# Rank sums in one PSUM column, edges and score rows requested sooner, eight loads and the exponential table begun ahead in a two-layer graph network kernel

## The chip, the cores and the metric

The kernel runs on one core of one Trainium2 chip. The metric is the device time of one execution in microseconds (us), the median over several runs. Engines are named as in the profile: PE (TensorE), PEld (its weight loads), DVE (VectorE), ACT (ScalarE), POOL (GpSimd) and SP (SyncE, which here only asks for transfers).

## The reference

There are 6250 nodes with 128 channels (x) and 200,000 edges (src, dst), sorted by dst. Two graph layers follow each other, each with a residual and a layer norm:

- Layer 0: the score of an edge is a · leaky_relu([x[src], x[dst]] w); its exponential is divided by the sum over the edges with the same src; the weighted rows x[src] are summed by dst.
- Layer 1: x is projected to 4 heads of 32 channels; the score of an edge is leaky_relu(left[src] + right[dst]) per head; a softmax runs over the edges with the same src; the rows of dst are summed by src; a projected residual is added and elu is applied.

## The kernel before

Nodes form 49 blocks of 128. For each block of dst the edges lie in one window of 128 x 36 entries. The kernel never gathers by index: it makes one-hot matrices and multiplies by them. Its stages come one after the other, each a block of instructions for all engines with a barrier behind it.

1. `load_and_place` (from line 2009) loads the constants and the first two windows of edges (L2032 and `load_windows`, L105), finds where each window starts, and lets ACT's queue ask for all of x (L2046, L2047).
2. `bin_windows` (from L114) sorts the edges of each of the 49 windows by block of src into slots of 128. Per window n, software-pipelined, DVE's order is: `find(n+2)` (block one-hot L202, equal keys L210 and L213), `pick(n+1)` (L223), `place(n)` (lane one-hot L238), once in seven windows `place_keys` (L187 to L194), `fold(n)` (payload, L245, two instructions), `sum_rank(n+1)` (L231). PE's order is: `fill(n-1)` (L317, 36 matmuls of 98 columns), `base(n+2)` (L278, 36 matmuls of 49 columns), `turn_x(n+2)` (L331), `take_off(n)` (L344), `rank(n+1)` (L288 to L306), `turn(n-1)` (L324), `project(n+1)` (L337). ACT's is: `measure_ranks` (L388), `take_raw` (L411, L412), `place_late` (L396), `take_base` (L382), `spread_key` (L372, L376), `take_x` (L425), `take_low` (L433), `spread_rank(n+1)` (L402), `take_bytes` (L418, L419), `take_high` (L429). SP stores the sorted rows of a window to DRAM (L167 to L171) and waits at the end of the stage until all stores have landed.
3. `score_edges` (from L467) computes the exponentials of layer 0 in 25 pairs of windows of 13 steps. SP loads the sorted rows, broadcast to all partitions, in groups (L564); DVE compares them with the partition number (L587).
4. `layer0_sums`, then `norm_and_project` (L1088 on), which norms the nodes, projects them for layer 1 and whose SP asks for the first `LOADS_1` = 3 groups of rows of layer 1 (L1083), then `layer1` (L1214 on): 343 steps; `make(u)` (L1262) turns a loaded group into one-hots, `add_scores` (L1386, L1388) sums scores, `exponent` (L1452) takes the exponential once a block's top is known, `weigh` (L1307) makes the messages.

The rank of an edge in its slot is the sum of two parts: what stands before it in other partitions, picked out of 49 counts, and how many equal keys stand before it in its own row of 36. `rank(n)` adds all of it by identity matmuls into a PSUM tile of 36 x 7 numbers, of which `sum_rank` then adds each seven:

```
for b in range(0, NB, SUB_B):
    w = min(SUB_B, NB - b)
    nc.tensor.matmul(rank_ps[:, :, 0:w], k.ident_b[:], picked[:, :, b:b + w], start=(b == 0), stop=False)
```

`picked` is laid out [128, 36, 49] in bf16, so two neighbours along its 36 are 98 bytes apart. The order of the work is written out by hand with semaphores; no planner is involved.

Of the kernel before, what the change touches and what calls it, by code (L numbers as in the profile page):

```python
# [18 lines left out]
P = 128  # L19
# [73 lines left out]
LOADS_1 = 3  # L93
# [15 lines left out]
def bin_windows(nc, k, PQ, rows, wide_rows, src_rows, X, src, dst):  # L109
    NB, RING, E = NBK, 3, dst.shape[0]  # L110
    LANE_G, BLK_G, SUB_B, SUB_T, SPREADS = 8, 7, 7, 6, 4
# [4 lines left out]
    with Stage(nc) as ctx:  # L116
# [10 lines left out]
        stored = [ctx.semaphore(f"bin_stored{h}") for h in range(2)]  # L127
# [17 lines left out]
        as_bytes, as_rows = sb("bytes", [P, 2, P], mybir.dt.uint8), sb("rows", [P, 2, P], BF16)  # L145
# [12 lines left out]
        with nc.Block() as block:  # L158
            @block.sync
            def _(sp):  # L160
# [3 lines left out]
                for n in range(NB):  # L164
                    sp.wait_ge(s["bytes"], n + 1)
# [6 lines left out]
                    if n % CHUNK == 0 and n // CHUNK + 2 < NB // CHUNK:  # L172
                        c = n // CHUNK + 2
                        sp.wait_ge(s["keyed"], c + 1)
                        load_windows(sp, k, src, dst, edges[:, c % 2], c * CHUNK, slice(0, CHUNK), read[c % 2])
                for h in range(2):
                    sp.wait_ge(stored[h], 80 * ((NB + 1 - h) // 2))

            @block.vector
            def _(dve):  # L180
# [45 lines left out]
                def sum_rank(n):  # L226
                    if n >= 2:
                        dve.wait_ge(s["rank_spread"], n - 1)
                        dve.wait_ge(s["away"], n - 1)
                    dve.wait_ge(s["ranked"], n + 1)  # L230
                    nc.vector.tensor_reduce(rank_sum[:, n % 2, :], rank_ps, AX.X, ALU.add).then_inc(s["rank_summed"], 1)  # L231

# [18 lines left out]
                place_keys(0, slice(0, FIRST), k.first_read, FIRST, k.first_edges)  # L251
                for n in range(-2, NB + 1):
                    if n + 2 < NB:
                        find(n + 2)
                    if 0 <= n + 1 < NB:
                        pick(n + 1)
# [9 lines left out]
                    if 0 <= n + 1 < NB:  # L266
                        sum_rank(n + 1)
# [4 lines left out]
            def _(pe):  # L272
# [8 lines left out]
                def rank(n):  # L281
# [4 lines left out]
                    for b in range(0, NB, SUB_B):  # L286
                        w = min(SUB_B, NB - b)
                        nc.tensor.matmul(rank_ps[:, :, 0:w], k.ident_b[:], picked[:, :, b:b + w], start=(b == 0), stop=False)  # L288
                    eq, counts = same[:, n % 2, :], rank_ps.rearrange("p t j -> p j t")
                    for t in range(0, 18, SUB_T):  # L290
                        nc.tensor.matmul(counts[:, 0:SUB_T, 18:36], k.ident_b[:],
                                         eq[:, t * W_T:(t + SUB_T) * W_T].rearrange("p (i t) -> p i t", t=W_T)[:, :, 18:36],
                                         start=False, stop=False)
                    halves = eq.rearrange("p (h x) -> p h x", h=2)
                    for t in range(0, 9, 3):
                        nc.tensor.matmul(counts[:, 0:3, :].rearrange("p j (h c) -> p h j c", h=2)[:, :, :, 9:18], k.ident_b[:],
                                         halves[:, :, t * W_T:(t + 3) * W_T].rearrange("p h (i t) -> p h i t", t=W_T)[:, :, :, 9:18],
                                         start=False, stop=False)
                    nines = eq.rearrange("p (h x) -> p h x", h=4)
                    for t in range(0, 6, 3):  # L300
                        nc.tensor.matmul(counts[:, 0:3, :].rearrange("p j (h c) -> p h j c", h=4)[:, :, :, t + 3:9], k.ident_b[:],
                                         nines[:, :, t * W_T:(t + 3) * W_T].rearrange("p h (i t) -> p h i t", t=W_T)[:, :, :, t + 3:9],
                                         start=False, stop=False)
                    threes = eq.rearrange("p (h x) -> p h x", h=12)
                    for t in range(2):
                        ins = nc.tensor.matmul(counts[:, 0, :].rearrange("p (h c) -> p h c", h=12)[:, :, t + 1:3], k.ident_b[:],  # L306
                                               threes[:, :, t * W_T + t + 1:t * W_T + 3], start=False, stop=(t == 1))
# [55 lines left out]
            def _(act):  # L363
                def spread_key(n):
                    if n in (0, FIRST, SECOND):
                        act.wait_ge(s["keyed"], 1 + (0, FIRST, SECOND).index(n))
                    elif n % CHUNK == 0:
                        act.wait_ge(s["keyed"], n // CHUNK + 3)
# [23 lines left out]
                def place_late(n):  # L392
# [3 lines left out]
                    nc.scalar.activation(lanes[:, EARLY:W_T], far[:], ACT.Relu, scale=-1.0, bias=k.one_col[:]).then_inc(s["late_lanes"], 1)  # L396

# [36 lines left out]

                spread_key(0)
                spread_key(1)
                for n in range(-2, NB + 1):
# [14 lines left out]
                    if 0 <= n + 1 < NB:  # L452
                        spread_rank(n + 1)
# [6 lines left out]
def score_edges(nc, k, PQ, rows, e0, den_out, flag, edges):  # L460
# [15 lines left out]
    with Stage(nc) as ctx:  # L476
# [9 lines left out]
        loaded = [ctx.semaphore(f"sc_loaded{h}") for h in range(2)]  # L486
        last_loaded = ctx.semaphore("sc_last_loaded")
        last_got = sb("last_rows", [P, R_BYTES], mybir.dt.uint8)
        got = k.spare_bytes[:, 0:2 * 8 * R_BYTES].rearrange("p (g c) -> p g c", g=2)
# [65 lines left out]
        with nc.Block() as block:  # L555
            @block.sync
            def _(sp):
                def load(pair, j, w, to, arrives):
                    of_rows = rows[pair, 16 * j:16 * j + 2 * w]
                    if pair == PAIRS - 1:  # L560
                        to = to.rearrange("p (a n l) -> p a n l", n=2, l=P)[:, :, 0, :]
                        sp.dma_start(to, of_rows[:, 0, :].partition_broadcast(P)).then_inc(arrives, 16)
                    else:
                        sp.dma_start(to, of_rows.rearrange("a n l -> (a n l)").partition_broadcast(P)).then_inc(arrives, 16)  # L564

                for pair in range(PAIRS):
                    for j in range(6):
# [4 lines left out]
                        load(pair, j, 8, got[:, j % 2], loaded[j % 2])  # L572
                    if pair >= 1:
                        sp.wait_ge(s["hot"], last_group_step(pair - 1, 6) + 1)
                    load(pair, 6, 1, last_got[:], last_loaded)
# [505 lines left out]
def load_rows(sp, k, got, wide_rows, u):  # L1081
    b, g = divmod(u, NBK // GX)
    sp.dma_start(got[:, u % LOADS_1].rearrange("p a x -> p (a x)"),  # L1083
                 wide_rows[g, 2 * b:2 * b + 2].rearrange("a i l -> (a i l)").partition_broadcast(P)
                 ).then_inc(k.rows_loaded[u % LOADS_1], 16)


def norm_and_project(nc, k, X, mean_var, hp, R, got, wide_rows):  # L1088
# [3 lines left out]
    with Stage(nc) as ctx:  # L1092
# [121 lines left out]
def layer1(nc, k, hp, got, wide_rows, spare, X, S, den4):  # L1214
    NB, PER, AHEAD = NBK, NBK // GX, 9
    R = NB * PER
    RING, LOADS = AHEAD + 2, LOADS_1
    CW, HP, FIRST = C + HEADS, 3 * HEADS, 28
    SPLIT, F32R = 3, mybir.dt.float32r
    with Stage(nc) as ctx:  # L1220
# [9 lines left out]
        loaded = k.rows_loaded  # L1230
# [3 lines left out]
        absent, never = sb("absent", [P, 2, NB], BF16), sb("never", [P, P], BF16)  # L1234
# [9 lines left out]
        with nc.Block() as block:  # L1244
            @block.sync
            def _(sp):
                for u in range(LOADS, R):
                    sp.wait_ge(s["hot"], u - LOADS + 1)
                    load_rows(sp, k, got, wide_rows, u)

            @block.vector
            def _(dve):
                ch = Chain(dve, s["chain"])

                def make(u):
                    dve.wait_ge(loaded[u % LOADS], 16 * (u // LOADS + 1))
# [1232 lines left out]
```

## Time and profile before

| | us |
|---|---|
| median of 3 runs | 3279.44 |
| lowest and highest | 3279.33, 3297.03 |
| the profiled execution | 3298.39 |
| its span | 3296.6 |

The page divides the span into 40 slices of 82.4 us. Sorting the windows fills the first five slices, the scores of layer 0 run up to the sixteenth, the sums of layer 0 to the twenty-seventh, layer 1 follows.

```profile
## 2 busy tenths in 40 slices
PE   5777699999999999699999999988999999999995
DVE  8999889999999997799999999988999999999996
ACT  6988788888888885799999999976888888888886
PEclk9988899999999997799999999998999999999998
```

Each digit is the busy share of a slice in tenths (9 is 90% or more); PEclk is the TensorE clock that was granted, in tenths of full speed.

### The profile page before, as it was taken

What the parts mean: (1) busy time and instruction counts of PE and PEld (TensorE: products, weight loads), DVE (VectorE), ACT (ScalarE), POOL (GpSimd) and SP (SyncE); (2) the same over time, 40 slices, a digit from 0 to 9 for tenths busy, and PEclk for the clock granted to TensorE, in tenths of its full rate; (3) what the DMA queues carried; (4) which work ended last, traced back from release to release, by engine and by line L of the source; (5) the groups of instructions that cost most, each with busy time, mean ns of one, the idle gap of its engine ahead of it and who ended that gap; (6) DMA issues with size and microseconds to landing.
All of it is one profiled execution on the core that took longest, in us unless ns stands there. A gap on an engine that the chain in (4) does not pass through costs nothing. (4 is left out here: it accounts for less than half of the span.)

```text
span 3296.6 us, 101505 instructions
## 1 busy us (share of the span) xinstructions
PE 3064.1 (93%) x40072; PEld 2795.8 (85%) x40072; DVE 3045.2 (92%) x4914; ACT 2749.8 (83%) x6951; POOL 155.1 (5%) x251
## 2 busy tenths in 40 slices
PE   5777699999999999699999999988999999999995
PEld 4666577777778777699999999988999999999993
DVE  8999889999999997799999999988999999999996
ACT  6988788888888885799999999976888888888886
POOL 0000000000000000000000000000111111111110
PEclk9988899999999997799999999998999999999998
DMA  2000022222222222233333333325554555555541
GB/s 66 13 13 12 10 103 93 92 86 92 93 91 93 92 87 47 65 97 97 97 97 97 96 97 96 97 58 162 161 163 160 163 163 161 162 164 163 160 141 41
DMA packets 173135, 333.06 MB, mean 101 GB/s; under 512 B 54860, under 2 KB 108704, under 8 KB 172576
## 3 DMA queue, kind: packets, MB, share of 16 engines
q1 hardware_dynamic: 170996, 323.30, 32.2%
q8 instruction: 322, 5.28, 0.6%
q10 hardware_dynamic: 1660, 3.20, 0.4%
q14 instruction: 157, 1.29, 0.1%
HBM read 320.77 MB, written 5.66 MB: 99 GB/s over the span
## 5 line engine op out<-in xcount | busy, mean ns | idle before, releaser
L987 PE MATMUL l_gathered<-xp,l_src_onehot 128*128 128x128 bf16 x7203 | 467.0, 221 | 11.2 <-DVE l_src_onehot L900 11.2
L1398 PE MATMUL l_gathered<-hp,l_onehot 128*128 128x128 bf16 x7203 | 458.9, 219 | 0.0
L682 PE MATMUL sc_z<-sc_onehot,pq 128*128 128x256 f32 (+1 forms) x2450 | 429.4, 298 | 27.6 <-DVE sc_leaky L595 18.3
L987 PEld LDWEIGHTS l_gathered<-xp,l_src_onehot 128*128 128x128 bf16 x7203 | 407.9, 99 | 26.4 <-DVE l_src_onehot L900 11.7
L766 ACT ACTIVATE sc_leaky<-sc_z 128x1024 f32<-128x1024 f32 (+3 forms) x325 | 309.4, 952 | 142.4 <-PE sc_z L686 139.5
L595 DVE SCALAR_TENSOR_TENSOR sc_leaky<-sc_z,sc_leaky 128x1024 f32<-128x1024 f32 (+3 forms) x325 | 370.1, 1139 | 59.9 <-ACT sc_leaky L766 52.3
L825 DVE TENSOR_TENSOR l_lane<-iota_b,l_lane_pairs 128x896 bf16<-128x896 bf16 x686 | 420.7, 613 | 0.0
L1398 PEld LDWEIGHTS l_gathered<-hp,l_onehot 128*128 128x128 bf16 x7203 | 406.6, 98 | 0.4
L686 PE MATMUL sc_z<-sc_onehot,pq 128*128 128x256 f32 (+1 forms) x2450 | 401.0, 286 | 0.0
L1412 PE MATMUL l_acc<-e,l_lane_wide 128*128 128x132 f32 x2744 | 385.3, 283 | 0.7 <-ACT e L1476 0.6
L682 PEld LDWEIGHTS sc_z<-sc_onehot,pq 128*128 128x128 f32 x2450 | 344.6, 196 | 40.2 <-issue 38.8
L686 PEld LDWEIGHTS sc_z<-sc_onehot,pq 128*128 128x128 f32 x2450 | 344.1, 195 | 0.0
L1307 DVE TENSOR_TENSOR e<-l_gathered,l_weight 128x768 f32<-128x768 f32 x343 | 325.5, 949 | 12.7 <-issue 9.0
L1412 PEld LDWEIGHTS l_acc<-e,l_lane_wide 128*128 128x128 f32 x2744 | 335.7, 190 | 1.6 <-ACT e L1476 1.0
L1465 ACT CAST l_lane_wide<-l_lane 128x896 fp32r<-128x896 bf16 x343 | 328.9, 959 | 0.0
L1033 ACT CAST l_lane_wide<-l_lane 128x896 fp32r<-128x896 bf16 x343 | 322.3, 940 | 4.0 <-DVE l_lane L825 4.0
L1470 ACT CAST l_message_halves<-e 128x396 fp32r<-128x396 f32 x343 | 179.1, 522 | 159.8 <-DVE e L1307 157.5
L998 PE MATMUL l_acc<-l_messages,l_lane_wide 128*128 128x128 f32 x2058 | 305.9, 285 | 5.7 <-ACT l_messages L1042 5.7
L587 DVE TENSOR_SCALAR sc_onehot<-placed,part 128x1536 fp32r<-128x1536 uint8 (+1 forms) x300 | 298.8, 997 | 3.4 <-DMA placed<-edge_rows 3.3
L1042 ACT ACTIVATE l_messages<-l_gathered,e 128x128 f32<-128x128 f32 x1029 | 300.5, 362 | 0.0
L914 DVE TENSOR_TENSOR l_message_halves<-l_messages,l_message_halves 128x512 fp32r<-128x512 f32 x343 | 237.3, 692 | 53.1 <-ACT l_message_halves L1048 48.0
L1476 ACT ACTIVATE e<-l_gathered,l_weight 128x32 f32<-128x32 f32 x1372 | 279.4, 285 | 0.0
(242 smaller groups left out, 6114.5 us busy)
## 6 DMA issues: line engine op xcount, KB each, us to landing
rows_got<-edge_rows_wide SPq DMA_DIRECT2D x343, 448.0 KB, 3.7
l_got<-edge_rows_src SPq DMA_DIRECT2D x343, 224.0 KB, 3.2
placed<-edge_rows SPq DMA_DIRECT2D x144, 512.0 KB, 3.7
out_dram<-X SPq DMA_DIRECT2D x12, 256.0 KB
edge_rows<-bin_bytes SPq DMA_DIRECT2D x98, 6.1 KB
edge_rows_wide<-bin_rows SPq DMA_DIRECT2D x98, 12.2 KB
sc_last_rows<-edge_rows SPq DMA_DIRECT2D x24, 64.0 KB, 3.5
placed<-edge_rows SPq DMA_DIRECT2D x6, 256.0 KB, 4.0
```

Source lines behind the costliest of these rows:

```text
L595: nc.vector.scalar_tensor_tensor(out=y, in0=z, scalar=ALPHA, in1=y, op0=ALU.mult, op1=ALU.add).then_inc(s["leaky"], 1)
L682: nc.tensor.matmul(z[:, b, 0:nw, :], PQ[:, b0 + b, q, 0:C], hot[:, r % HOTS, b, 0, 0:nw, :], start=(b == u and q == 0), stop=False)
L686: ins = nc.tensor.matmul(z[:, u:u + v, n, :], PQ[:, 2 * pair + n, q, C:2 * C], hot[:, r % HOTS, u:u + v, 1, n, :], start=False, stop=(n == ...
L766: nc.scalar.activation(y, z, ACT.Relu, scale=1.0 - ALPHA).then_inc(s["positive"], 1)
L825: return nc.vector.tensor_tensor(out.rearrange("p i (u v) -> p i u v", v=2), k.iota_b[:].rearrange("p (u v) -> p u v", v=2).unsqueeze(1).t ...
L987: ins = nc.tensor.matmul(gps[:, t % 2, i * P:(i + 1) * P], hot[:, t % RING, i, :], parts[:, g * GX + i, q, :], start=(q == 0), stop=(q == 2))
L998: nc.tensor.matmul(acc[:, n % 2, 0:C], lane_wide[:, t % 2, i, :].bitcast(F32), msg[:, t % 2, i, :], start=(g == 0 and i == SPLIT), stop=Fa ...
L1033: nc.scalar.copy(lane_wide[:, t % 2], lane[:, t % 2]).then_inc(s["lane_wide"], 1)
L1307: nc.vector.tensor_tensor(msg[:, t % 2, 0:w, 0:C].rearrange("p i (e d) -> p i e d", e=HEADS), gps[:, t % 2, 0:w * P].rearrange("p (i e d) ...
L1398: ins = nc.tensor.matmul(gps[:, t % 2, i * P:(i + 1) * P], dst_hot[:, t % RING, i, :], hp[:, g * GX + i, q, 0:C], start=(q == 0), stop=(q ...
L1412: nc.tensor.matmul(acc[:, b % 2, 0:CW], lane_wide[:, t % 2, i, :].bitcast(F32), msg[:, t % 2, i, :], start=(g == 0 and i == SPLIT), stop=F ...
L1465: nc.scalar.copy(lane_wide[:, t % 2], lane[:, t % 2]).then_inc(s["lane_wide"], 1)
```

## The change

In `bin_windows` the rank sums go into one number per edge: 49 + 18 + 9 + 6 + 2 = 84 matmuls of 12 to 36 columns in place of 17 of 12 to 252; `sum_rank` on DVE goes, and ACT copies the 36 sums out of PSUM (`take_rank`) ahead of `spread_rank`. The first window's keys are placed as soon as that window is there; x is asked for in two parts, the first seven blocks in the first stage and the rest by ACT's queue at the start of `bin_windows`. SP asks for the first two groups of score rows ahead of the last window's stores, and the wait for those stores moves into the scoring stage, ahead of pair 22. `norm_and_project` asks for eight groups of layer 1, five of them into a part of S that is written only later; `layer1` opens with one exponential of a constant column on ACT.

```diff
-        rank_ps = ps("rank_ps", [P, 512])[:, 0:SUB_B * W_T].rearrange("p (t j) -> p t j", j=SUB_B)
+        rank_ps = ps("rank_ps", [P, 512])[:, 0:W_T]
...
                 for n in range(NB):
+                    if n == NB - 1:
+                        sp.wait_ge(s["key_spread"], NB)
+                        sp.wait_ge(s["spread"], NB)
+                        sp.wait_ge(s["same"], NB)
+                        for h in range(2):
+                            sp.wait_ge(stored[h], 80 * (NB // 2))
+                        for j in range(2):
+                            load_score_rows(sp, k, rows, 0, j, 8, score_rows(k)[:, j], k.score_rows[j])
                     sp.wait_ge(s["bytes"], n + 1)
...
-                for h in range(2):
-                    sp.wait_ge(stored[h], 80 * ((NB + 1 - h) // 2))
...
-                def sum_rank(n):
...
-                    nc.vector.tensor_reduce(rank_sum[:, n % 2, :], rank_ps, AX.X, ALU.add).then_inc(s["rank_summed"], 1)
...
-                place_keys(0, slice(0, FIRST), k.first_read, FIRST, k.first_edges)
+                place_keys(0, slice(0, 1), k.zero_read, 1, k.first_edges)
                 for n in range(-2, NB + 1):
                     if n + 2 < NB:
                         find(n + 2)
+                    if n == -2:
+                        place_keys(0, slice(1, FIRST), k.first_read, FIRST - 1, k.first_edges)
...
-                    for b in range(0, NB, SUB_B):
-                        w = min(SUB_B, NB - b)
-                        nc.tensor.matmul(rank_ps[:, :, 0:w], k.ident_b[:], picked[:, :, b:b + w], start=(b == 0), stop=False)
-                    eq, counts = same[:, n % 2, :], rank_ps.rearrange("p t j -> p j t")
-                    for t in range(0, 18, SUB_T):
...
+                    for b in range(NB):
+                        nc.tensor.matmul(rank_ps, k.ident_b[:], picked[:, :, b], start=(b == 0), stop=False)
+                    eq = same[:, n % 2, :]
+                    for t in range(18):
+                        nc.tensor.matmul(rank_ps[:, 18:36], k.ident_b[:], eq[:, t * W_T + 18:t * W_T + 36], start=False, stop=False)
...
                 def turn_x(n):
                     if n == 0:
+                        pe.wait_ge(k.x_first, 16)
+                    if n == CHUNK:
                         pe.wait_ge(k.x_loaded, 32)
...
+                def take_rank(n):
+                    if n >= 2:
+                        act.wait_ge(s["rank_spread"], n - 1)
+                        act.wait_ge(s["away"], n - 1)
+                    act.wait_ge(s["ranked"], n + 1)
+                    nc.scalar.copy(rank_sum[:, n % 2, :], rank_ps).then_inc(s["rank_summed"], 1)
...
+                full = x.shape[0] // P
+                act.dma_start(X[:, CHUNK:full, :], x[CHUNK * P:full * P].rearrange("(b p) c -> p b c", p=P)).then_inc(k.x_loaded, 16)
                 spread_key(0)
...
                     if 0 <= n + 1 < NB:
+                        take_rank(n + 1)
                         spread_rank(n + 1)
...
+def rows_ahead(S):
+    return S[:, 10:45, :].rearrange("p b c -> p (b c)").bitcast(BF16).rearrange("p (u a x) -> p u a x", u=AHEAD_1, a=2)
...
-                for u in range(LOADS_1):
-                    load_rows(sp, k, got, wide_rows, u)
+                for u in range(LOADS_1 + AHEAD_1):
+                    load_rows(sp, k, got, S, wide_rows, u)
...
-                for u in range(LOADS, R):
-                    sp.wait_ge(s["hot"], u - LOADS + 1)
-                    load_rows(sp, k, got, wide_rows, u)
+                for u in range(LOADS_1 + AHEAD_1, R):
+                    turn = (u - LOADS_1 - AHEAD_1) // LOADS_1
+                    sp.wait_ge(s["hot"], u - LOADS_1 + 1 if turn else u - LOADS_1 - AHEAD_1 + 1)
+                    load_rows(sp, k, got, S, wide_rows, u)
...
+                nc.scalar.activation(exp_ready[:], k.one_col[:], ACT.Exp)
                 find_absent(0)
...
-                act.dma_start(X[:, 0:NFULL, :], x[0:NFULL * P].rearrange("(b p) c -> p b c", p=P)).then_inc(k.x_loaded, 16)
+                act.dma_start(X[:, 0:CHUNK, :], x[0:CHUNK * P].rearrange("(b p) c -> p b c", p=P)).then_inc(k.x_first, 16)
```

## Rows read from the trace of the kernel before

**Rows 1.** The page: busy time over the span, share of it, instructions.

```profile
PE 3064.1 (93%) x40072; PEld 2795.8 (85%) x40072; DVE 3045.2 (92%) x4914; ACT 2749.8 (83%) x6951; POOL 155.1 (5%) x251
```

**Rows 2.** Windows: stretch, its length, busy (instructions) per engine, PEclk, DMA share, GB/s.

```profile
165.00:247.00 82.00, 60.95 (x991) 52.93 (x991) 81.25 (x102) 71.80 (x236) 0.00 (x0) 0.90 0.08 13
```

**Rows 3.** Timeline of DVE, one window sorted: start, length, engine, line, operation.

```profile
152.72 0.41 DVE L231 TENSOR_REDUCE bin_rank_sum<-bin_rank_ps 128x36 f32<-128x252 f32 x1
153.05 1.19 DVE L202 TENSOR_TENSOR bin_onehot<-iota_b,e 128x1764 bf16<-128x1764 bf16 x1
...
155.82 2.01 DVE L238 TENSOR_TENSOR bin_lanes<-iota_b,bin_rank 128x3584 bf16<-128x3584 bf16 x1
...
159.99 0.41 DVE L231 TENSOR_REDUCE bin_rank_sum<-bin_rank_ps 128x36 f32<-128x252 f32 x1
```

**Rows 4.** Timeline of DVE: the first and the last of the 49 L202.

```profile
22.72 1.21 DVE L202 TENSOR_TENSOR bin_onehot<-iota_b,e 128x1764 bf16<-128x1764 bf16 x1 [1.07 <-ACT e L372]
...
381.16 1.20 DVE L202 TENSOR_TENSOR bin_onehot<-iota_b,e 128x1764 bf16<-128x1764 bf16 x1
```

**Rows 5.** Timeline of PE, the same window; in brackets the idle time before.

```profile
153.05 1.78 PE L317 MATMUL bin_slots<-bin_payload,bin_lanes 128*128 128x98 bf16 x36 [2.07 <-DVE bin_payload L245]
154.68 1.10 PE L278 MATMUL bin_base<-bin_onehot,above_b 128*128 128x49 bf16 x36
155.61 0.30 PE L331 MATMUL bin_x_turned_ps<-ident,X 128*128 128x128 f32 x1
...
156.00 1.13 PE L288 MATMUL bin_rank_ps<-bin_picked,ident_b 128*128 128x252 bf16 x7
156.96 0.44 PE L291 MATMUL bin_rank_ps<-bin_same,ident_b 128*128 128x108 bf16 x3
...
157.53 0.24 PE L324 MATMUL bin_turned<-ident_b,bin_raw 128*98 128x128 bf16 x1
157.60 0.65 PE L337 MATMUL bin_product<-w_ext,bin_x_turned 128*128 128x256 f32 x2
```

**Rows 6.** Timeline of ACT, the same window.

```profile
153.22 0.38 ACT L402 CAST bin_rank<-bin_rank_sum 128x224 bf16<-128x224 f32 x1 [0.49 <-DVE bin_rank_sum L231]
...
157.82 0.21 ACT L382 CAST bin_base_sum<-bin_base 128x49 bf16<-128x49 f32 x1
```

**Rows 7.** Timelines of PE and of DVE at the lower clock.

```profile
169.63 3.10 PE L317 MATMUL bin_slots<-bin_payload,bin_lanes 128*128 128x98 bf16 x36 [4.11 <-DVE bin_payload L245]
...
172.77 2.03 DVE L238 TENSOR_TENSOR bin_lanes<-iota_b,bin_rank 128x3584 bf16<-128x3584 bf16 x1 [0.30 <-PE bin_slots L317]
```

**Rows 8.** Timelines of ACT and DVE, and windows, at the start of the sorting.

```profile
14.42 1.28 ACT L372 ACT_TABLE_LOAD   x1 [6.72 <-PEq L60]
...
20.37 0.20 DVE L187 TENSOR_SCALAR bin_block_of<-e 128x72 int32<-128x72 int32 x1 [5.65 <-DMA e<-in_dst_dram]
...
33.18 2.02 DVE L238 TENSOR_TENSOR bin_lanes<-iota_b,bin_rank 128x3584 bf16<-128x3584 bf16 x1
...
16.00:18.00 2.00, 0.00 (x0) 0.00 (x0) 0.00 (x0) 0.00 (x0) 0.00 (x0) 1.00 1.06 285
```

**Rows 9.** From sorting to scoring: timeline of DVE; SP's waits (total, times, longest).

```profile
414.68 1.95 DVE L587 TENSOR_SCALAR sc_onehot<-placed,part 128x1536 fp32r<-128x1536 uint8 x2 [3.32 <-DMA placed<-edge_rows]
...
SPq L158 <- DMA edge_rows_src<-bin_rows: 0.9, 1, 0.9
```

**Rows 10.** Start of layer 1: DVE's waits for its loads; timelines of ACT and DVE.

```profile
DVE l_onehot L1262 <- DMA rows_got<-edge_rows_wide: 7.3, 7, 2.3
...
2252.53 1.28 ACT L1452 ACT_TABLE_LOAD   x1
...
2254.39 0.96 DVE L1307 TENSOR_TENSOR e<-l_gathered,l_weight 128x768 f32<-128x768 f32 x1 [0.47 <-ACT l_weight L1452]
```

**Rows 11.** Windows: the end of the scoring.

```profile
1290.00:1300.00 10.00, 10.00 (x65) 8.74 (x67) 4.46 (x10) 5.14 (x18) 0.00 (x0) 0.50 0.22 34
```

More of the change, by code:

```diff
@@ L92 @@
 GX = 7
-LOADS_1 = 3
+LOADS_1, AHEAD_1 = 3, 5
 R_BYTES = 4 * P
@@ L144, in bin_windows @@
         raw = sb("raw", [P, 2, 2 * NB], BF16)
-        as_bytes, as_rows = sb("bytes", [P, 2, P], mybir.dt.uint8), sb("rows", [P, 2, P], BF16)
+        late = e0[:].rearrange("p a b -> p (a b)")[:, 2304:2496]
+        as_bytes = late[:, 0:64].bitcast(mybir.dt.uint8).rearrange("p (h l) -> p h l", h=2)
+        as_rows = late[:, 64:192].bitcast(BF16).rearrange("p (h l) -> p h l", h=2)
         xt = sb("x_turned", [P, 2, C])
         base_ps = ps("base", [P, 512])[:, 0:NB]
-        rank_ps = ps("rank_ps", [P, 512])[:, 0:SUB_B * W_T].rearrange("p (t j) -> p t j", j=SUB_B)
+        rank_ps = ps("rank_ps", [P, 512])[:, 0:W_T]
         slots_ps = ps("slots", [P, 512])[:, 0:2 * NB]
@@ L294, in rank @@
+                    eq = same[:, n % 2, :]
+                    for t in range(18):
+                        nc.tensor.matmul(rank_ps[:, 18:36], k.ident_b[:], eq[:, t * W_T + 18:t * W_T + 36], start=False, stop=False)
                     halves = eq.rearrange("p (h x) -> p h x", h=2)
[L295 to L298, printed above, removed]
+                    for t in range(9):
+                        nc.tensor.matmul(rank_ps.rearrange("p (h c) -> p h c", h=2)[:, :, 9:18], k.ident_b[:],
+                                         halves[:, :, t * W_T + 9:t * W_T + 18], start=False, stop=False)
@@ L299, in rank @@
                     nines = eq.rearrange("p (h x) -> p h x", h=4)
[L300 to L303, printed above, removed]
+                    for t in range(6):
+                        c = t // 3 * 3 + 3
+                        nc.tensor.matmul(rank_ps.rearrange("p (h c) -> p h c", h=4)[:, :, c:9], k.ident_b[:],
+                                         nines[:, :, t * W_T + c:t * W_T + 9], start=False, stop=False)
@@ L557, in _ @@
             def _(sp):
[L558 to L564, printed above, removed]
                 for pair in range(PAIRS):
-                    for j in range(6):
+                    if pair == PAIRS - 3:
+                        for h in range(2):
+                            sp.wait_ge(k.stored[h], 80 * ((NB + 1 - h) // 2))
+                    for j in range(2 if pair == 0 else 0, 6):
                         if pair >= 1 or j >= 2:
@@ L571, in _ @@
                             sp.wait_ge(s["away"], late_steps(used + 1))
-                        load(pair, j, 8, got[:, j % 2], loaded[j % 2])
+                        load_score_rows(sp, k, rows, pair, j, 8, got[:, j % 2], loaded[j % 2])
                     if pair >= 1:
                         sp.wait_ge(s["hot"], last_group_step(pair - 1, 6) + 1)
-                    load(pair, 6, 1, last_got[:], last_loaded)
+                    load_score_rows(sp, k, rows, pair, 6, 1, last_got[:], last_loaded)
             @block.vector
@@ L1255, in make @@
                 def make(u):
-                    dve.wait_ge(loaded[u % LOADS], 16 * (u // LOADS + 1))
+                    rows, arrived, count = place_of_rows(k, got, S, u)
+                    dve.wait_ge(arrived, count)
                     if u >= RING:
```

76 lines of the change are left out of this document (43 added, 33 removed).

## Prediction

> **What bounds the kernel now.** The page first: PE and DVE are each busy for over nine tenths of the span [rows 1], so no one engine is the answer and each stage must be read by itself. The change touches one long stage, the sorting of the 49 windows, and three seams: the start, the step from sorting to scoring, the start of layer 1. The sums of layer 0 and the body of layer 1 are left as they are. In the sorting stage DVE is busy for 81.25 of 82 us, PE for 61 and ACT for 72 [rows 2]: DVE bounds it. The timeline of one window shows how. DVE comes round in 159.99 - 152.72 = 7.27 us with no gap [rows 3]; PE is idle for 2.07 us of that, waiting for the payload [rows 5], and ACT for 0.49 us, waiting for the rank sum [rows 6]. Over the stage, with the keys of a new chunk in every seventh window, the mean is (381.16 - 22.72) / 48 = 7.47 us [rows 4].
>
> **The rank sum leaves DVE.** L231 runs 0.41 us but the next instruction starts 0.33 us behind it [rows 3], so 0.33 us is what it costs. It goes 49 times. Twice at the end and once at the start DVE waits for another engine just behind it, so I count 46: 46 x 0.33 = **15.2 us**, if neither PE nor ACT takes over at 7.27 - 0.33 = 6.94 us.
>
> ACT gets a copy out of PSUM much like L382, 0.21 us [rows 6], and `spread_rank` must wait for its result, so I charge 0.25 us. ACT's round is 7.27 - 0.49 + 0.25 = 7.03 us. That is over 6.94 in a plain window and under the mean of 7.47 - 0.33 = 7.14. It may slip by 0.09 us in each of six windows and catches up when DVE places keys. `place` reads the spread rank about 2.2 us after it is made now (155.82 against 153.22 + 0.38) [rows 3, 6], so the slip is covered: nothing. The copy stands where the wait stood, and PE has the sum ready long before (157.53 against ACT's arrival near 160).
>
> PE is the open question. The rank matmuls take 157.53 - 156.00 = 1.53 us now; seven wide ones take 0.96 of it, 137 ns each for 252 columns [rows 5]. Afterwards 49 matmuls read 36 columns each, every column 98 bytes from the last, and 35 more read short contiguous stretches. For the 35 I take 26 ns each, the spacing of L278 ((155.61 - 154.68) / 36) [rows 5]: 0.91 us. The 49 are not in the trace. Their lower bound is the same 26 ns. Their upper bound is 137 ns: L288 too makes 36 jumps of 98 bytes, and picks up seven columns after each. Between them I reason from what L288 pays for its jumps. L317 streams 98 columns in (154.68 - 153.05) / 36 = 45 ns, 0.46 ns a column, so 252 columns should take 116 ns, or 105 at 2.4 GHz; the excess is 21 to 32 ns for 36 jumps. Add 36 columns (17 or 15 ns) and a narrow one costs 38 to 47 ns; I take 45, near the upper of the two. The rank part is then 49 x 0.045 + 0.91 = 3.1 us, up 1.6.
>
> Does PE still fit? From L317's start to the end of L337 it now spends 5.2 us [rows 5], of which 0.3 is a wait for `pick` that DVE's earlier arrival removes. The rest without rank is 5.2 - 0.3 - 1.53 = 3.35 us, so the round is 4.26 + 49c, with c the price of a narrow matmul in us. At c = 0.045 it is 6.46, under 6.94 by 0.48; PE takes over at c = 55 ns. The 67 extra weight loads run beside the matmuls, as in L278's spacing.
>
> The slack is thin where the clock is low. The granted clock is 0.90 on average in this stage [rows 2], so the lower of the two levels (1.2 of 2.4 GHz) holds for a fifth of it. There L317 takes 3.10 us instead of 1.78, and DVE already waits 0.30 us for it [rows 7]. A fifth of 350 us at half speed is up to 35 us of PE work that comes late. PE's idle 2.07 us a window swallows that today; afterwards 49 x 0.48 = 23 us of slack are left, so at most 12 us come through. With PE idle for less of each window the clock may also fall less often, which would make it nothing. I take off **5 us**, a little under the middle.
>
> The Trainium skill speaks against this part. Its page "SBUF — State Buffer", section "Door 1: The DMA port swizzle", says that reads run at full rate only while they stay in a 16-byte line, at least two to a line, and that each step to a new line pays. Each column here is in a line of its own. The 137 ns of L288 agree that jumps cost; the page has no size for it. Its page "TensorE: Matmul & The Clock Gate", section "Wait — 56ns, not 53.3ns?", gives a floor of about 25 ns however narrow; by that alone all 84 would take an estimated 2.1 us and the 5 us above would mostly stay.
>
> **The start.** DVE sits idle for 5.65 us until the second window of edges lands at 20.37 [rows 8]. The new code places the first window at 14.5, but ACT first issues a transfer and loads its table (1.28 us, from 14.42) [rows 8], so it can spread keys only near 16.6, and `find(0)` starts near 17.7 in place of 22.7. Placing keys in two parts and waiting for ACT between them gives back 2.5 us. The later windows, asked for from 15.3 on, now queue with the 2.7 MB of x that were issued beside them; at 285 GB/s [rows 8] that is 9.5 us, so windows 2 and 3 land near 25.5 when DVE wants them at 24.5. I find the first `place` near 31.0 against 33.18 [rows 8]: **2.2 us**, between 1 and 3.3 (queue hides nothing or costs nothing).
>
> **From sorting to scoring.** DVE waits 3.32 us for the first rows, and SP had waited 0.9 us for the last stores to land before anyone could leave the stage [rows 9]. Both go: **4.2 us**. The two loads (512 KB each) are asked for near 404 and land near 408, before DVE is ready. SP's new waits stand ahead of the last window's stores, but all they wait for is over before those rows exist near 407, so nothing queued behind is late. The moved wait for the stores is met hundreds of us earlier: nothing. Late next is the start of the constants and barriers, which stays.
>
> **Start of layer 1.** DVE waits 7.3 us in all for its first loads, 6.7 of it ahead of the first block's top [rows 10]. With eight there these waits go. But ACT now loads the table before it finds the absent slots, which PE's first scores wait for: 0.7 us late. The table load of 1.28 us stands on the path to the first weights at 2254.39 [rows 10] and leaves it; the gather that ends near 2253.1 allows 1.2 of it. Together 6.7 - 0.7 + 1.2 = 7.2; I take **7.0 us**, between 6 and 8. Five more issues on SP and 2.2 MB more lie in the projection stage, where the core moves almost nothing. Later loads are asked for by the same rule as before.
>
> **Sum.** 15.2 - 5 + 2.2 + 4.2 + 7.0 = 23.6 us. The profiled execution took 3298.4 (span 3296.6), so it would take 3274.8. It stood 19 us above the median of the runs; from that median, 3279.4 - 23.6 = **3255.8 us**. A measurement of this kernel can tell about 1% (33 us) from no change, so this is "within 1%".
>
> **Rivals.**
> - *PE takes over and the kernel gets slower.* Place: the 49 narrow matmuls. The seams give 13.4 us, 0.27 a window, so the loss begins where 4.26 + 49c passes 7.47 + 0.27, at c = 71 ns. Halfway between my 45 and the bound of 137, at c = 90 ns, the round is 8.67 us: 49 x 1.20 = 59 us lost, less 13.4, gives 3279.4 + 45.4 = 3325. For it: the jumps and L288's price. Against it: 36 columns are a seventh of L288's. Chance 0.12. By the SBUF page's rule this is the direction. Between 55 and 71 ns the time lies from 3262 to 3279: 0.16.
> - *The clock decides the rest.* PE is full for 10 us of 10 at half clock at the end of the scoring [rows 11]. The runs differ by 17.7 us (3297.03 against 3279.33). If the moved seams put most runs in the longer case, the median is 3255.8 + 18 = 3274: 0.12.
> - *Everything goes well.* PE's slack holds and each seam gives its upper value: 15.2 + 3.3 + 4.2 + 8 = 30.7, so 3249, and a little less if low-clock waits of today go too: 0.12.
> - Forecast, 3250 to 3262: 0.48.
>
> **Range and chances.** 3247 to 3286 takes in the forecast, the good case, the clock case and the balanced PE; it leaves out the dear narrow matmul. Faster by over 1% (under 3246.6) needs more than all upper values: 0.10. Slower by over 1% (over 3312) needs c above 85 ns: 0.10. Within 1%: 0.80.
>
> **What would show it.** Right: L231 gone, DVE's round 6.9 to 7.0 us in plain windows; the spacing of the 36-column matmuls near 45 ns; PE's wait for the payload down to about 0.5 us; DVE's gap ahead of L187 under 1 us; no wait of DVE for the first score rows; the first weights of layer 1 in ACT without a table load. Wrong: a spacing above 55 ns, with DVE waiting for `bin_slots` in most windows; a long wait for windows 2 and 3 behind x; table loads that come back between the first exponential and the weights.

## The result, and the profile after

The kernel became slower: 3388.0 us (median of 5 runs, 3384.1 to 3391.0) against 3279.4 (5 runs), a ratio of 1.032 with a 95% interval of 1.030 to 1.035. The profiled execution took 3387.84, its span 3386.0; the one of before took 3298.39, 19 us above its median, and this execution holds those 19 us in one place, the scoring (last section).

First the page of after: busy time over the span, and the slices, to be read against [rows 1] and the slices of before.

```profile
PE 3263.5 (96%) x43355; PEld 3018.4 (89%) x43355; DVE 3041.4 (90%) x4872; ACT 2771.9 (82%) x7001; POOL 154.2 (5%) x251
...
PE   7999998999999999889999999998999999999995
...
DVE  7777777999999999889999999997999999999997
...
PEclk8666668999999999889999999998999999999998
```

PE has 199 us more to do and DVE 4 us less. Sorting now fills over six slices in place of nearly five; in them DVE is at 0.7 and PE full, and the granted clock, 0.9 and 0.8 before, is 0.6. The windows of after over the stretch of [rows 2] say the same (stretch, length, busy and instructions of PE, PEld, DVE, ACT, POOL, PEclk, DMA share, GB/s). The second row lies on the 36 matmuls of one `fill`:

```profile
165.00:247.00 82.00, 82.00 (x1292) 78.78 (x1290) 59.65 (x64) 57.67 (x186) 0.00 (x0) 0.67 0.06 11
...
159.30:162.30 3.00, 3.00 (x38) 3.00 (x37) 0.85 (x1) 2.89 (x11) 0.00 (x0) 0.50 0.09 17
```

PE is busy for 82.00 of 82 us where it was for 60.95. One window in the timeline of DVE (start, length, engine, line, operation; in brackets the idle time before and what ended it):

```profile
152.24 2.03 DVE L252 TENSOR_TENSOR bin_lanes<-iota_b,bin_rank 128x3584 bf16<-128x3584 bf16 x1 [2.33 <-PE bin_slots L327]
...
158.41 0.33 DVE L231 TENSOR_TENSOR bin_same<-e,placed 128x324 bf16<-128x324 bf16 x1 [0.61 <-PE bin_rank_ps L316]
...
159.06 1.09 DVE L244 TENSOR_TENSOR bin_picked<-bin_onehot,bin_base_sum 128x1764 bf16<-128x1764 bf16 x1
162.49 2.02 DVE L252 TENSOR_TENSOR bin_lanes<-iota_b,bin_rank 128x3584 bf16<-128x3584 bf16 x1 [2.33 <-PE bin_slots L327]
```

DVE comes round in 162.49 - 152.24 = 10.25 us, where it took 7.27 without a gap [rows 3]. The reduction is gone, and two waits for PE stand in the round: 2.33 us for `fill`, 0.61 us for `rank`. The timeline of PE shows what they wait for, to be held against [rows 5]:

```profile
153.35 4.09 PE L301 MATMUL bin_rank_ps<-bin_picked,ident_b 128*128 128x36 bf16 x49
157.26 0.65 PE L304 MATMUL bin_rank_ps<-bin_same,ident_b 128*128 128x18 bf16 x18
...
158.34 1.17 PE L349 MATMUL bin_product<-w_ext,bin_x_turned 128*128 128x256 f32 x2
159.30 3.15 PE L327 MATMUL bin_slots<-bin_payload,bin_lanes 128*128 128x98 bf16 x36
162.25 1.24 PE L292 MATMUL bin_base<-bin_onehot,above_b 128*128 128x49 bf16 x36
```

No bracket is left: PE never waits. The 49 narrow matmuls stand (157.26 - 153.35) / 49 = 80 ns apart. The 36 of `fill` take 3.15 us in each of the windows between 67 and 380 us, at a granted clock of 0.50, where most took 1.78 before [rows 5]. In steps of 1 us the clock is 1.00 over the first of the narrow matmuls (163.20 to 165.20), 0.50 from 166.20 on, through the last third of them, `project` and `fill`, and on the way up again (0.79 from 162.20 to 163.20) while `base` runs. The waits of `place` between 40 and 380 us, in total, times and longest, say how general this is:

```profile
DVE bin_lanes L252 <- PE bin_slots L327: 70.7, 34, 2.3
```

From the first `place` to the end of the last payload it is 524.16 - 30.95 = 493.2 us, against 402.17 - 33.18 = 369.0: **124.2 us lost**, 2.53 in each of 49 windows. The seams, of DVE's and ACT's timelines after, to be held against [rows 8 to 10]:

```profile
25.06 0.20 DVE L208 TENSOR_SCALAR bin_block_of<-bin_edges 128x72 int32<-128x72 int32 x1 [1.00 <-DMA bin_edges<-in_dst_dram]
...
30.95 2.02 DVE L252 TENSOR_TENSOR bin_lanes<-iota_b,bin_rank 128x3584 bf16<-128x3584 bf16 x1
...
532.28 1.02 DVE L604 TENSOR_SCALAR sc_onehot<-placed,part 128x1536 fp32r<-128x1536 uint8 x1
...
2345.85 0.46 ACT L1483 ACTIVATE l_weight<-l_score,l_negated 128x196 f32<-128x196 f32 x1
...
2346.57 0.96 DVE L1338 TENSOR_TENSOR e<-l_gathered,l_weight 128x768 f32<-128x768 f32 x1
```

The first `place` stands at 30.95 and stood at 33.18: 2.2 us. From the last payload to the first make of the scores it is 532.28 - 524.16 = 8.1 us in place of 414.68 - 402.17 = 12.5: 4.4. From the start of the norm (2293.74, before 2194.10) to the first messages it is 52.8 us in place of 60.3: 7.5, and the exponential at 2345.85 has no table load ahead of it. Against the median of before, 124.2 - 2.2 - 4.4 - 7.5 = 110 us; measured were 108.6.

### The profile page after: what moved, and what is told of

It is laid out like the page before. It is cut to its first block and busy times, and to the rows that moved or that the text cites. A ratio compares the mean times of both kernels' runs of the same rounds, so it can differ in the third digit from the quotient of the medians.

```text
span 3386.0 us, 108082 instructions
## 1 busy us (share of the span) xinstructions
PE 3263.5 (96%) x43355; PEld 3018.4 (89%) x43355; DVE 3041.4 (90%) x4872; ACT 2771.9 (82%) x7001; POOL 154.2 (5%) x251
## 5 line engine op out<-in xcount | busy, mean ns | idle before, releaser
L699 PE MATMUL sc_z<-sc_onehot,pq 128*128 128x256 f32 (+1 forms) x2450 | 419.7, 293 | 23.2 <-DVE sc_leaky L612 18.0
L1004 PEld LDWEIGHTS l_gathered<-xp,l_src_onehot 128*128 128x128 bf16 x7203 | 407.9, 99 | 26.3 <-DVE l_src_onehot L917 11.7
L703 PE MATMUL sc_z<-sc_onehot,pq 128*128 128x256 f32 (+1 forms) x2450 | 393.9, 282 | 0.0
L699 PEld LDWEIGHTS sc_z<-sc_onehot,pq 128*128 128x128 f32 x2450 | 334.5, 191 | 35.4 <-issue 34.1
L703 PEld LDWEIGHTS sc_z<-sc_onehot,pq 128*128 128x128 f32 x2450 | 338.1, 192 | 0.0
L1338 DVE TENSOR_TENSOR e<-l_gathered,l_weight 128x768 f32<-128x768 f32 x343 | 326.0, 950 | 12.5 <-issue 9.0
```

What stands on the lines that cost most here:

```text
L699: nc.tensor.matmul(z[:, b, 0:nw, :], PQ[:, b0 + b, q, 0:C], hot[:, r % HOTS, b, 0, 0:nw, :], start=(b == u and q == 0), stop=False)
L703: ins = nc.tensor.matmul(z[:, u:u + v, n, :], PQ[:, 2 * pair + n, q, C:2 * C], hot[:, r % HOTS, u:u + v, 1, n, :], start=False, stop=(n == ...
L1004: ins = nc.tensor.matmul(gps[:, t % 2, i * P:(i + 1) * P], hot[:, t % RING, i, :], parts[:, g * GX + i, q, :], start=(q == 0), stop=(q == 2))
L1338: nc.vector.tensor_tensor(msg[:, t % 2, 0:w, 0:C].rearrange("p i (e d) -> p i e d", e=HEADS), gps[:, t % 2, 0:w * P].rearrange("p (i e d) ...
```

## The experiments

Theory A: a narrow matmul is dear because each of its columns lies in another small piece of SBUF (the chip's on-chip memory, from which PE reads); PE becomes the bound, and its clock, which falls in this stage, makes it worse. Rivals: the number of matmuls or their weight loads is what costs (B); a seam hurts something later (C).

**Each half by itself.** `seams_only` keeps the sums and `sum_rank` of before; `rank_only` is before with the new sums alone.

```diff
 # seams_only: after, but (shortened)
-        rank_ps = ps("rank_ps", [P, 512])[:, 0:W_T]
+        rank_ps = ps("rank_ps", [P, 512])[:, 0:SUB_B * W_T].rearrange("p (t j) -> p t j", j=SUB_B)
...
-                        take_rank(n + 1)
+                        sum_rank(n + 1)
```

> The changed kernel with the rank sums as they were (17 wide matmuls and the sum on DVE); all of the seams stay changed. If the loss is all in the rank sums, the seams give what their rows show after the change (2.2 us at the start, 4.4 from sorting to scoring, 7.5 at the start of layer 1): 3279.4 - 14 = 3265, and the sorting goes back to 7.27 us a plain window. If the seams carry part of the loss (x asked for in two parts, loads ahead of the last stores), the time is above 3279.

> The kernel before with the rank sums of the changed one alone. If the rank sums carry all of the loss and the seams are apart from it: 3388 + 14 = 3402, windows of 10.25 us as in the changed kernel. If the two work on each other (the earlier start shifting the clock, say), it differs from that by more than 5 us.

Measured: seams only 3265.4 us (10 runs, 3264.4 to 3267.1) against 3279.1, ratio 0.9945 (0.9926 to 0.9965); rank only 3403.8, ratio 1.036 (1.032 to 1.040). So the seams give 13.7 and the sums cost 124.7; together 111, near the 108.6 of the whole. That speaks against C: nothing later is hurt. In seams only the stretch of [rows 2] reads as before:

```profile
165.00:247.00 82.00, 62.69 (x1033) 54.52 (x1034) 81.58 (x95) 72.35 (x235) 0.00 (x0) 0.90 0.08 14
```

Seams only is also the fastest version here, half a per cent under before, with an interval that leaves out 1.

**The price of a jump, by itself.** `step_probe` adds rows of 48 equal matmuls on a zeroed tile to the first stage of the kernel before, one row for each step between columns. (One execution, 3308.4 us, of which only these rows are read.) In short form, not the code itself, with columns, step of reading and step of writing:

```diff
+ for cols, step, out in [(128,1,1),(36,1,1),(36,2,1),(36,4,1),(36,8,1),(36,16,1),(36,49,1),(18,49,1),(72,8,1),(36,1,7),(72,1,7),(128,1,1)]:
+     for _ in range(48):
+         nc.tensor.matmul(tried[cols, out elements apart], k.ident_b[:], zero[cols, step elements apart], start=True, stop=True)
```

> The kernel before with series of 48 extra matmuls at the end of the first stage, each of a row of zeros, with one price to read from each: the spacing. Theory A (each new 16-byte piece of SBUF that the moving operand touches costs a fixed 2.2 ns): 36 columns that lie 2, 4, 8, 16, 32, 98 bytes apart take 26, 26, 40, 80, 80, 80 ns, 18 columns 98 bytes apart take 40, 72 columns 16 bytes apart 160. Theory B (any step over one element costs the same): 80 ns from 4 bytes on. Theory C (a matmul in a long row of narrow ones pays a fixed sum): 18 columns cost as much as 36. PSUM columns written 28 bytes apart: 30 ns for 36 and 60 for 72, if 0.84 ns a column from the rank sums of before holds. The whole time only shows the series' own length, some 30 to 40 us more.

Measured, in the timeline of PE (two bytes an element; the order is that of the list):

```profile
16.61 1.36 PE L2122 MATMUL tried_psum<-tried_zero,ident_b 128*128 128x36 bf16 x48
17.81 1.35 PE L2124 MATMUL tried_psum<-tried_zero,ident_b 128*128 128x36 bf16 x48
19.01 1.85 PE L2126 MATMUL tried_psum<-tried_zero,ident_b 128*128 128x36 bf16 x48
20.69 1.77 PE L2128 MATMUL tried_psum<-tried_zero,ident_b 128*128 128x36 bf16 x24
23.06 1.76 PE L2128 MATMUL tried_psum<-tried_zero,ident_b 128*128 128x36 bf16 x24 [0.60 <-issue]
24.65 3.44 PE L2130 MATMUL tried_psum<-tried_zero,ident_b 128*128 128x36 bf16 x48
27.91 4.02 PE L2132 MATMUL tried_psum<-tried_zero,ident_b 128*128 128x36 bf16 x48
31.75 2.42 PE L2134 MATMUL tried_psum<-tried_zero,ident_b 128*128 128x18 bf16 x48
33.99 6.42 PE L2136 MATMUL tried_psum<-tried_zero,ident_b 128*128 128x72 bf16 x48
...
42.90 3.17 PE L2140 MATMUL tried_psum<-tried_zero,ident_b 128*128 128x72 bf16 x48
45.87 2.88 PE L2142 MATMUL tried_psum<-tried_zero,ident_b 128*128 128x128 bf16 x48
```

From one row's start to the next, divided by 48 (for 16 bytes by 24, from 23.06 to 24.65), 36 columns cost 25 ns when 2 or 4 bytes apart, 35 at 8 bytes, 66 at 16, 68 at 32 and 80 at 98. At 16 and 32 bytes that is about 1.9 ns a column, at 98 bytes 2.2; 18 columns at 98 bytes cost 47 ns and 72 columns at 16 bytes 130. The unit that fits is a piece of 16 bytes: with 8 bytes between columns there are half as many new pieces, and half the price (35 for 18 pieces). The fixed 2.2 ns that I had expected for each piece does not hold: it gave 80 ns at 16 and 32 bytes, 40 for the 18 columns and 160 for the 72. Why 98 bytes cost more than 32 stays open.

The price doesn't depend on the clock. The two groups of 24 at 16 bytes run at 0.96 and at 0.50, and take 1.77 and 1.76 us; the 36 columns at 98 bytes lie in the third of these windows, at 0.50, and cost the same 80 ns at 1.00 (next experiment):

```profile
20.70:22.30 1.60, 1.60 (x29) 1.58 (x25) 0.00 (x0) 0.00 (x0) 0.00 (x0) 0.96 0.04 12
23.10:24.60 1.50, 1.50 (x24) 1.50 (x25) 0.00 (x0) 0.00 (x0) 0.00 (x0) 0.50 0.04 11
28.00:36.00 8.00, 8.00 (x114) 7.93 (x112) 0.00 (x0) 0.00 (x0) 0.00 (x0) 0.50 0.01 2
```

The Trainium skill ("SBUF — State Buffer", section "Door 1: The DMA port swizzle") says that a read pays for each new 16-byte line. The trace agrees with the 16 bytes. The same section says that two hits in a line are enough for the full rate and that a stride of 8 bf16 is free; for a matmul's moving operand the trace doesn't agree: at two a line the price is 35 ns against 25, at 8 bf16 it is 66.

**The same price, added to the kernel before.** Three kernels add 49 matmuls a window, whose results nobody reads, ahead of the old rank sums (`flat` is `picked` as one row of 1764): 36 columns 98 bytes apart, 36 side by side, or 180 side by side.

```diff
                     for b in range(NB):
+                        nc.tensor.matmul(rank_all[:, 256:292], k.ident_b[:], picked[:, :, b], start=True, stop=True)         # extra_apart
+                        nc.tensor.matmul(rank_all[:, 256:292], k.ident_b[:], flat[:, 36 * b:36 * b + 36], start=True, stop=True)   # extra_close
+                        nc.tensor.matmul(rank_all[:, 256:436], k.ident_b[:], flat[:, 32 * b:32 * b + 180], start=True, stop=True)  # extra_wide
```

> The kernel before, with DVE's rank sum and its wide matmuls kept, and 49 narrow matmuls more in each window that read 36 columns 98 bytes apart into PSUM that nobody reads. It asks for the price of the narrow matmuls without any change of DVE or ACT. By the probe 49 x 0.080 = 3.9 us; PE's round is 4.9 + 3.9 = 8.8 us at full clock, over the mean of 7.47, which gives 3279 + 49 x 1.35 = 3345; if the clock falls as in the changed kernel (10.25 us where 8.2 was its full-clock sum), a round is about 10.9 and the time 3447.

> The same with 49 narrow matmuls that read 36 neighbouring columns: as many instructions, as many columns, only the step differs. If the step is the price: 49 x 0.025 = 1.2 us, PE's round 6.1 us stays under DVE's 7.27, granted clock near 0.9 or above, 3279 to 3285. If 49 more short matmuls are the price whatever they read, it is as slow as its twin with the step, near 3447.

> The same with 49 matmuls of 180 neighbouring columns, which at full clock take as long as the strided ones (about 78 ns): PE is as busy, but streams five times the columns. If the clock in the sorting follows what is streamed and not how long PE is busy, it stays near 1.0 here and the time is 3279 + 49 x 1.25 = 3340, about 100 us under the twin with the step. If a longer PE round by itself lowers the clock, it falls here too and the time is above 3450.

Measured: apart 3415.3 us, ratio 1.041 (1.038 to 1.044); close 3282.8, ratio 1.0005 (0.9985 to 1.0025); wide 3356.3, ratio 1.023 (1.020 to 1.026). The spacings were 79, 25 and 77 ns. The windows of the three, in this order:

```profile
165.00:247.00 82.00, 82.00 (x1149) 75.58 (x1147) 60.88 (x72) 54.29 (x177) 0.00 (x0) 0.83 0.06 10
```

```profile
165.00:247.00 82.00, 70.33 (x1468) 62.38 (x1467) 80.56 (x99) 71.00 (x232) 0.00 (x0) 0.94 0.08 15
```

```profile
165.00:247.00 82.00, 81.41 (x1309) 75.90 (x1307) 69.51 (x81) 62.42 (x203) 0.00 (x0) 1.00 0.06 11
```

Close against before: 2401 more matmuls and weight loads cost nothing, since PE is still idle for 11.7 of 82 us. So B falls. Apart against wide: nearly the same time per matmul, but 59 us between the two. The 2 ns make 49 x 49 x 0.002 = 5 us of it, and the rest, 54 us, goes with the clock, 0.83 against 1.00. PE is at work all the time in both. So a matmul that waits for its columns doesn't only take PE's time, it also leaves the matmuls around it at a lower clock. My forecasts for the two missed by 16 to 70 us: they let the clock cost either everything or nothing. The rows of one window of `extra_apart` show both kinds of matmul, the narrow ones at the full clock and the old wide ones behind them at the lower:

```profile
202.85 4.08 PE L288 MATMUL bin_rank_ps<-bin_picked,ident_b 128*128 128x36 bf16 x49
206.74 1.66 PE L291 MATMUL bin_rank_ps<-bin_picked,ident_b 128*128 128x252 bf16 x7
208.21 0.73 PE L294 MATMUL bin_rank_ps<-bin_same,ident_b 128*128 128x108 bf16 x3
...
202.90:206.70 3.80, 3.80 (x50) 3.80 (x50) 3.80 (x3) 3.73 (x11) 0.00 (x0) 1.00 0.09 14
206.80:208.20 1.40, 1.40 (x9) 0.89 (x7) 0.00 (x0) 0.00 (x0) 0.00 (x0) 0.50 0.22 26
```

At 1.00 the narrow ones stand (206.74 - 202.85) / 49 = 79 ns apart, as at 0.50 in the probe.

**Taking the jumps away.** `close_layout` and `seven_layout` are after with another order of `picked`: 36 neighbours of one block side by side, or stretches of seven blocks.

```diff
-        picked = sb("picked", [P, W_T, NB], BF16)
+        picked = sb("picked", [P, NB, W_T], BF16)                    # close_layout
+        picked = sb("picked", [P, NB // BLK_G, W_T, BLK_G], BF16)    # seven_layout
```

> The changed kernel with the picked counts laid out so that the 36 columns of a narrow matmul are neighbours; DVE writes them 72 bytes apart instead. All 84 narrow matmuls stay. Theory A (the step is the price): their spacing falls from 80 to 26 ns, the clock comes back to 0.9 or more in the sorting, PE waits for DVE again. DVE's pick then may lose its faster mode: 1764 elements at one a cycle are about 1.84 us in place of 1.09, so a mean window of 7.14 + 0.75 = 7.9 us: 3279.4 - 14 + 49 x 0.42 = 3286; if DVE isn't slowed, 3250. Rival (the number of matmuls is the price): spacing and clock stay, 3388 or more.

> The changed kernel with the picked counts laid out so that the 36 columns lie 14 bytes apart, 32 pieces of 16 bytes instead of 36; DVE writes them in stretches of seven. By the probe (67 ns for 36 pieces at steps of 16 bytes, 35 ns for 18) a narrow matmul takes 60 to 65 ns in place of 80, PE's round at full clock 4.26 + 49 x 0.063 = 7.3 us. If the price goes by pieces and the clock recovers, 3275 to 3300; if the clock stays near 0.6, 3330 to 3350. If any step costs the same, 3388. DVE's scattered write may cost more than its 1.09 us: at 4.4 ns for each separate stretch (the neighbouring-columns layout cost 7.87 us for 1764) it would be about 1.2 us for 252 stretches.

Measured: close layout 3579.8 us, ratio 1.090 (1.086 to 1.095). Its matmuls and its `pick`, in the timelines of PE and of DVE:

```profile
156.72 1.63 PE L301 MATMUL bin_rank_ps<-bin_picked,ident_b 128*128 128x36 bf16 x49 [4.89 <-issue]
...
162.56 7.88 DVE L244 TENSOR_TENSOR bin_picked<-bin_onehot,bin_base_sum 128x1764 bf16<-128x1764 bf16 x1
```

The matmuls are 30 ns apart at a clock of 0.50, near the 26 that A expected. The other half of that expectation failed: the clock in the stretch of [rows 2] is 0.62, not 0.9 or more, though PE is idle for 34 of its 82 us. And the layout that is good for PE is bad for DVE: writing every result 72 bytes from the last takes 7.88 us in place of 1.09, and DVE's round is 13.8 us. I had put the write at 1.84 us and missed it by four times. The kernel shows the price of the jumps and not what their absence would give.

Seven layout is the compromise. It took 3300.4 us (8 runs, four of them 3289.6 to 3291.0 and four 3309.9 to 3312.1), ratio 1.0045 (1.001 to 1.008). DVE's `pick` and PE's rank sums:

```profile
155.64 3.06 PE L301 MATMUL bin_rank_ps<-bin_picked,ident_b 128*128 128x36 bf16 x49 [0.35 <-issue]
...
161.48 1.71 DVE L244 TENSOR_TENSOR bin_picked<-bin_onehot,bin_base_sum 128x1764 bf16<-128x1764 bf16 x1
```

Its windows:

```profile
165.00:247.00 82.00, 78.20 (x1603) 74.94 (x1601) 79.36 (x85) 69.42 (x229) 0.00 (x0) 0.90 0.09 15
```

With columns 14 bytes apart the spacing is (158.52 - 155.64) / 49 = 59 ns. That too speaks for the piece and against a price for each jump: there are 36 jumps, as at 16 bytes, but only about 32 pieces, 1.8 ns each. The clock is back at 0.90, and PE is busy for 78 of 82 us: 88 us of the 108.6 are gone by the median, 98 by the lower four runs, though `pick` costs 0.62 us more a window (30 us). The lower four runs stand 25 us over the seams alone. The dearer `pick` less the reduction that is gone makes 30 - 15 = 15 of it, and DVE's waits for PE between 40 and 380 us, 8.0 us in all, most of the rest.

**The clock, put back.** `filler` is after with 14 wide matmuls a window, whose results nobody reads, between the narrow ones.

```diff
                         nc.tensor.matmul(rank_ps, k.ident_b[:], picked[:, :, b], start=(b == 0), stop=False)
+                        if b % 7 in (2, 6):
+                            nc.tensor.matmul(filler[:, 0:180], k.ident_b[:], flat[:, 32 * b:32 * b + 180], start=True, stop=True)
```

> The changed kernel with 14 matmuls of 180 neighbouring columns strewn among the 49 strided ones of each window, into PSUM that nobody reads: 14 x 0.077 = 1.1 us of work more. PE's round at full clock is 8.2 + 1.1 = 9.3 us. If the changed kernel's other 1.7 us a window (9.94 measured, 8.2 at full clock) are the clock, and the clock follows what PE streams, it comes back towards 1.0 and the round falls to 9.3 to 9.6: 3355 to 3370, faster than 3388 with more work. If the clock doesn't come back, the round is 9.94 + 1.1 or more: 3440. If the 1.7 us are no clock matter at all: also 3440.

Measured: 3413.8 us, ratio 1.041 (1.039 to 1.043). Its windows and one `fill`:

```profile
165.00:247.00 82.00, 82.00 (x1401) 78.70 (x1400) 59.61 (x65) 56.65 (x186) 0.00 (x0) 0.83 0.06 11
...
165.22 2.06 PE L329 MATMUL bin_slots<-bin_payload,bin_lanes 128*128 128x98 bf16 x36
```

This fell between the two expectations, and 26 us above after. But 19 of these are not in the sorting: from the first make of the scores to the step behind the stage it is 911.2 us in filler's profiled execution and 892.2 in after's, a difference that before has too (last section). Without it filler stands 7 us above after. The clock rose from 0.67 to 0.83 and `fill` went from 3.15 us to 2.06, though PE was full in both kernels. DVE's round is 171.67 - 161.42 = 10.25 us, as in after: 14 x 0.077 = 1.08 us of added work took back what the clock gave. It shows that the clock follows what PE does between, and that its share is about this large; it gives no gain. A kernel with the narrow sums at the full clock and no added work was not run.

## Why the prediction was wrong

**The price of the narrow matmul** failed first. I took 45 ns, measured were 80. My upper bound of 137 held. The thresholds that I had drawn, PE takes over at 55 ns and the loss begins at 71, were not tried between: at 80 ns PE bounds the stage, and seven layout, where PE nearly fits at 59, has a DVE round longer by 0.62 us. The mistake is in how L288 was read. I took its 137 ns, subtracted the time of streaming 252 columns (105 to 116 ns) and called the rest the price of 36 jumps. That supposes that the two add up. The runs say that they go on beside each other and the longer one counts: 36 stretches of 14 bytes lie in about 1.75 pieces of 16 bytes each, 63 in all; 137 / 63 = 2.2 ns a piece, and 36 x 2.17 = 78 ns for the narrow matmul. At the lower clock the same wide matmuls of `extra_apart` stand (208.21 - 206.74) / 7 = 210 ns apart, which is the time of their 252 columns at 1.2 GHz, with nothing on top for the jumps. The row [rows 5] had held the answer.

**The clock** was the larger miss in microseconds. With c = 80 ns my own sum gives a round of 4.26 + 49 x 0.080 = 8.18 us, so 49 x (8.18 - 7.47) = 35 us over before, and with the seams a time of 3301. The stage lost 124; the other 89 us come from PE's work at the lower clock, 0.67 of the full one on average where it was 0.90. The rows of one window bear that out: `fill` takes 162.25 - 159.30 = 2.95 us where it took 1.63, `base` 163.33 - 162.25 = 1.08 for 0.93, and `project` 1.17 for 0.65. Together that is 2.0 us of the 2.07 by which the round of 10.25 exceeds 8.18. I had charged 5 us, and said that with less idle time the clock might fall less often. The opposite happened: PE never idles and the clock is lower. The argument held only for matmuls that read side by side (0.94 in close and 1.00 in wide against 0.90). Before, the falls lay under PE's idle 2.07 us; with PE the bound nothing hides them. That the clock costs this kind of amount is shown (apart against wide, 54 us at 0.83); the exact split of 124 into 35 and 89 is a sum, since no run had the narrow sums at the full clock.

**The 15.2 us of the rank sum** never came, since DVE waits for PE in 34 of the windows looked at. DVE did lose the instruction; in seven layout, where PE nearly fits, DVE waits for it in few windows, but there the dearer `pick` takes more than the 15 us, so no run shows the gain. **ACT's copy** takes 0.19 us, and `spread_rank` starts 158.76 - 158.49 = 0.27 us behind its start, where I had charged 0.25; it stands where ACT's wait stood.

**The seams** were right: 2.2 (2.5 without the new sums, where the first `place` of seams only stands at 30.69), 4.4 and 7.5 us against 2.2, 4.2 and 7.0, and 13.7 by themselves against a sum of 13.4. The wait for windows of edges behind x is there, 1.00 us at 25.06. DVE no longer waits for the loads of layer 1, where it had waited 7.3 us [rows 10], and the exponential has no table load.

**The rivals.** "PE takes over" was the right one, with its place; at its c = 90 ns it gave 3325, still 63 too little, because it too had left the clock as it was. I gave it 0.12. The bounds for c went up to 137 ns, and between ends that far apart I had trusted a difference of two near numbers. "The clock decides the rest" told of another stage, and its 18 us did not come in after's five runs.

## What to carry to other kernels

Count the 16-byte pieces that the moving operand of a matmul (the one that it streams through) touches, at 1.8 to 2.6 ns each in these runs: the matmul takes that or its streaming time, whichever is longer, so a view that picks one element out of each row of a tile costs as much as reading far more of it. Before work is moved from a bound engine to PE, ask what the clock will be once PE has no idle time: a PE full of narrow, waiting matmuls may be given the lower clock, at which `fill` and `project` took 1.8 times as long here. When a layout is changed to suit the reader, price the writer too.

## What had not been expected of the hardware

- PE can be busy for 82.00 of 82 us at a clock of 0.67, and at 0.50 for 8 of 8 us in the probe; with 49 matmuls of 180 columns a window (extra_wide) it was 1.00 over 82 us, of which PE was busy for 81.41.
- The price of a jump is the same at both clocks (36 columns 98 bytes apart: 79 ns at 1.00 and 80 at 0.50).
- Writing to PSUM has its own step price: 72 columns written 28 bytes apart from contiguous input stand (45.87 - 42.90) / 48 = 62 ns apart at a clock of 1.00, more than the 128 columns written side by side in the row behind them (48 in 2.88 us). The Trainium skill ("SBUF — State Buffer", section "Door 1: The DMA port swizzle") says that matmuls are slowed by any PSUM pattern that isn't contiguous, and here it agrees.
- DVE's 1764 bf16 results take 1.09 us side by side, 1.71 in stretches of seven and 7.88 us when each is 72 bytes from the last, 4.5 ns each.
- At the start of an execution the matmuls don't bear out the clock that the windows give. Ahead of after's first narrow matmuls it reads 1.00, but `base` takes 1.68 us, where it takes 1.10 at 1.00 in [rows 5]; before has the same 1.68 at 23.99, with the DMA engines nearly idle (0.13):

```profile
22.46 1.68 PE L292 MATMUL bin_base<-bin_onehot,above_b 128*128 128x49 bf16 x36 [1.99 <-DVE bin_onehot L223]
...
22.50:24.20 1.70, 1.70 (x37) 1.66 (x38) 1.56 (x3) 0.00 (x0) 0.00 (x0) 1.00 1.10 270
```

- The 19 us of before's profiled execution lie at the end of the scoring. From the first make of the scores to the step behind the stage it is 911.2 us before and 892.2 after. In the stretch at the stage's end before was at the lower clock; the second row is the same stretch of after, 117.6 us later:

```profile
1272.00:1350.00 78.00, 60.88 (x511) 49.03 (x510) 48.15 (x83) 33.89 (x78) 0.00 (x0) 0.50 0.16 36
...
1389.60:1467.60 78.00, 52.09 (x585) 43.72 (x578) 59.78 (x99) 47.31 (x108) 0.00 (x0) 0.73 0.20 45
```

This comes in some executions and not in others: four of 15 runs of before on one chip stood at 3298 to 3300 and the rest at 3278 to 3281, none of the ten of seams only, and four of eight of seven layout. The profiled executions of seven layout (3311.8 us) and of filler have it too, with the same 911.2 us. What starts it was not tried.
